# One step for each stage on each engine, and all steps placed anew, in a fused attention and expert kernel

## The reference: what is computed

```python
x = x + xattn(layernorm(x), ctx)   # 16 heads of 32; the context is key and value, then one 512 x 512 projection
x = x + attn(layernorm(x), ...)    # low-rank q, k, v with a rotation, 16 heads, 32 x 32 scores, projection
x = x + ffn(layernorm(x), ...)     # 8 experts: argmax of a gate picks one expert per row; GELU between two 512 x 512 layers
```

## Time and profile before

| what | value |
|---|---|
| median of three runs | 898.3 us |
| profiled execution: own time, span | 901.93 us, 900.0 us |
| TensorE busy, mean granted clock | 773.6 us (86% of the span), 0.926 |
| VectorE, ScalarE, GpSimd busy | 604.1, 422.1, 319.6 us |
| first scores to last scores of the 64 batches | 10.0 to 647.8 us |
| last tile's stages, then the routing | to about 714 us |
| experts | to the end, 900 us |

### The profile page before, as it was taken

The page is one execution under the profiler, slowest core; times in us unless marked ns, Lnnn a source line. Parts: engine busy times, 40 slices in busy tenths (PEclk is TensorE's granted clock), DMA queues, the critical chain, the costliest instruction groups (busy, mean ns, idle before and its releaser), DMA issues.

```text
span 900.0 us, 26139 instructions
## 1 busy us (share of the span) xinstructions
PE 773.6 (86%) x10442; PEld 573.5 (64%) x10442; DVE 604.1 (67%) x1195; ACT 422.1 (47%) x1063; POOL 319.6 (36%) x638
## 2 busy tenths in 40 slices
PE   4896988979788897978889797888979888999998
PEld 3543756758566675757667585766767665566664
DVE  3476766767776676677676677767654645678883
ACT  2353454544644455454645455454541344555552
POOL 2013333223333323233332223333230234776652
PEclk9998898989898898989889898988989889999999
DMA  9955455546646463554645465374250199654430
GB/s 265 314 133 101 135 120 119 146 98 135 151 107 145 118 154 105 121 130 96 173 114 136 98 154 130 97 176 110 35 193 32 52 355 393 210 170 141 149 120 4
DMA packets 113848, 129.05 MB, mean 143 GB/s; under 512 B 13950, under 2 KB 80766, under 8 KB 113728
## 3 DMA queue, kind: packets, MB, share of 16 engines
q1 hardware_dynamic: 105984, 109.26, 46.6%
q0 software_dynamic: 5520, 16.26, 5.3%
q10 hardware_dynamic: 2224, 1.86, 0.8%
HBM read 114.76 MB, written 14.42 MB: 144 GB/s over the span
## 4 chain that ended last, share of the span: by engine, by line
PE 55%; DVE 14%; issue 10%; POOL 8%; ACT 7%; SPq 3%; DMA 2%; ACTq 0%; POOLq 0%; DVEq 0%
PE bank L497 11%; PE bank L498 8%; PE bank L499 8%; PE bank L1551 7%; PE scores L548 3%; PE scores L538 3%; PE bank L562 3%; PE bank L491 3%; ACT prob L813 2%; POOL operand_lo L1283 2%; DVE k_block L1114 2%; PE scores L1529 2%; PE scores L1531 2%; PE scores L1530 2%; PE bank L602 2%
## 5 line engine op out<-in xcount | busy, mean ns | idle before, releaser
L813 ACT ACTIVATE prob<-scores,negmax 128x257 f32<-128x257 f32 x256 | 118.0, 476 | 85.0 <-DVE negmax L1021 84.7
L548 PE MATMUL scores<-consts,prob 128*128 128x128 f32 x512 | 89.5, 303 | 60.7 <-ACT prob L813 60.7
L1021 DVE TENSOR_REDUCE negmax<-scores 128x2 f32<-128x514 f32 x128 | 82.0, 682 | 67.4 <-PE scores L538 67.4
L548 PEld LDWEIGHTS scores<-consts,prob 128*128 128x128 f32 x512 | 67.5, 156 | 73.4 <-ACT prob L813 68.1
L497 PE MATMUL bank<-qkv_hi,operand_hi 128*128 128x396 f32 x256 | 100.1, 391 | 3.9 <-DVE operand_lo L1025 3.8
L1011 DVE STREAM_TRANSPOSE k_t<-keys 128x512 f32<-128x512 f32 x128 | 88.1, 690 | 3.1 <-DMA keys<-in_ctx 3.0
L498 PE MATMUL bank<-qkv_lo,operand_hi 128*128 128x396 f32 x256 | 89.0, 348 | 0.1
L499 PE MATMUL bank<-qkv_hi,operand_lo 128*128 128x396 f32 x256 | 88.7, 347 | 0.0
L1551 PE MATMUL bank<-w_all,hidden 128*128 x184 | 82.8, 592 | 0.6 <-ACT hidden L1604 0.6
L562 PEld LDWEIGHTS bank<-prob_t,context 128*32 128x32 f32 x4096 | 48.7, 115 | 45.5 <-issue 45.2
L1647 DVE TENSOR_TENSOR w_lo<-w_all,w_hi 128x512 fp32r<-128x512 f32 x89 | 69.5, 839 | 0.1
(11 more groups left out here) (245 smaller groups left out, 1743.2 us busy)
## 6 DMA issues: line engine op xcount, KB each, us to landing
keys<-in_ctx SPq DMA_DIRECT2D x256, 128.0 KB, 4.6
context<-in_ctx SPq DMA_DIRECT2D x64, 512.0 KB, 4.7
w_all<-in_L_ffn_W SPq DMA_DIRECT2D x16, 1024.0 KB, 10.2
b<-in_L_ffn_b SPq DMA_DIRECT2D x23, 256.0 KB
norm_scratch<-norm SPq DMA_DIRECT2D x16, 256.0 KB, 2.0
x_tile<-in_x SPq DMA_DIRECT2D x8, 256.0 KB, 4.8
x_pair<-in_x SPq DMA_DIRECT2D x8, 256.0 KB, 4.8
x_scratch<-x_tile SPq DMA_DIRECT2D x8, 256.0 KB, 2.6
```

Of the source, the lines that this page charges most:

```text
L548: done = pe.transpose(scores[:, 2 * pair, at:at + P], prob[pair][:, gg, c * P:(c + 1) * P], ident)
L813: act.activation(prob[pair][:, gg, :], scores[:, g, 0:J], ACT.Exp, bias=negmax[b % 2][:, g:g + 1], accum_out=sums[t % 2][:, g, bl:bl + 1]) ...
L1021: dve.tensor_reduce(negmax[b % 2][:, 2 * pair:2 * pair + 2], scores[:, 2 * pair:2 * pair + 2, 0:J], AX.X, ALU.max, negate=True).then_inc(m ...
```

## The change

The table of constants gets a step of its own for each stage on each engine, and parts that were spread over steps in a row (`XOUT`, `OUT`, `SOFT_PLACE`) get a tuple of steps. The fixed distances (`QKV + 4`, `TURN_Q + 1`, `AV + 2`, `RANK + 1`) are gone. All numbers are new, those inside a batch too. Which heads of k ScalarE and VectorE place is now in two names, with the values as before. No instruction is added or removed in the 16 tiles, and the code of each stage is the same.

```diff
-(INVERT, SPREAD_INV, SPREAD_LAST, WEIGH_LAST, X_BIAS, ATT, ATT_INV, ATT_HI, ATT_LO, XOUT, X1, SCALE1, TURN1, QKV, OUT_BIAS, TURN_Q, TURN_K,
- SELF, SOFT, SOFT_EXP, SOFT_SUM, SOFT_SCALE, SOFT_TURN, SOFT_PLACE, AV, OUT, X2, SCALE3, TURN3, GATE, CHOOSE, RANK,
- QUERIES) = (
-    -5, -3, 0, 1, -6, 2, 3, 4, 4, 8, 17, 19, 21, 24, 26, 41, 41, 45, 46, 46, 50, 48, 56, 55, 63, 83, 89, 86, 95, 105, 105, 118, -54)
-MEASURE_X, SCALE_X = 2 * STEPS + 4, 2 * STEPS + 5
-LATER = {"OUT": (6, 0), "X2": (12, 0), "SCALE3": (25, 8), "TURN3": (36, 0), "GATE": (28, 0), "CHOOSE": (29, 0), "RANK": (17, 0)}
+INVERT, SPREAD_INV, SPREAD_LAST, WEIGH_LAST = -5, -4, 1, -3
+ATT, ATT_INV, ATT_HI, ATT_LO = 5, 6, 4, 12
+X_BIAS, XOUT, X1, ROOT1, SCALE1 = -28, (8, 9, 11, 13), 16, 20, 18
+TURN1, NORM_HI, NORM_LO = 21, 19, 19
+QKV = tuple(range(24, 40))
+QKV_MOVE, ROTATE, OUT_BIAS = (28, 31, 36, 40), 30, 21
+TURN_Q, Q_MOVE, TURN_K, K_PLACE, K_PLACE_DVE = 44, 44, 41, 41, 45
+SELF, SOFT, SOFT_EXP, SOFT_SUM, SOFT_SCALE, SOFT_TURN, SOFT_PLACE = 46, 49, 49, 50, 56, 56, (53, 55, 60, 62)
+AV, SELF_HI, SELF_LO, OUT, X2, ROOT3 = 66, 66, 70, (81, 85, 86, 87), 89, 85
+SCALE3, TURN3, X3_MOVE, GATE, CHOOSE, RANK, RANKED = 90, 95, 96, 105, 105, 120, 120
+QUERIES, QUERIES_MOVE = -55, -54
+MEASURE_X, ROOT_X, SCALE_X = 25, 26, 30
+LATER = {'OUT': (16, -4), 'X2': (19, 0), 'SCALE3': (26, 12), 'TURN3': (29, 7), 'GATE': (38, 14), 'CHOOSE': (31, 4), 'RANK': (25, 1)}
...
-KEYS_AT = (5, 7)
-KEYS_LOAD_AT = 6
-TURN_P_AT = (6, 8)
-ATTEND_AT = (10, 12)
-KEEP_AT = (7, 9)
+KEYS_AT = (6, 7)
+KEYS_LOAD_AT = 8
+TURN_P_AT = (7, 8)
+ATTEND_AT = (10, 11)
+KEEP_AT = (7, 8)
...
-def part_at(step, offset, parts, later=(0, 0)):
-
-    for part in range(parts):
-        t = tile_at(step, offset + part, later)
+def part_at(step, offsets, later=(0, 0)):
+
+    for part, offset in enumerate(offsets):
+        t = tile_at(step, offset, later)
         if t >= 0:
             return t, part
     return -1, 0
...
-            t = tile_at(step, TURN_Q + 1)
+            t = tile_at(step, Q_MOVE)
             if t >= 0:
                 until.wait_ge(q_turned, t + 1)
...
-            t = tile_at(step, TURN_K + 1)
-            if t >= 0:
+            t = tile_at(step, K_PLACE_DVE)
+            if t >= 0 and DVE_K:
...
-            t = tile_at(step, X2, LATER["X2"])
+            t = tile_at(step, ROOT3, LATER["X2"])
             if t >= 0:
                 root("r", measured_r, t + 1, normed_r, rstd_r)
```

More of the change, by code:

```diff
@@ L367, in program @@
     bank_of = {"queries": 0, "xout": 0, "norm": 1, "qkv0": 1, "qkv2": 1, "out": 2, "gate": 0, "av": 0, "qkv1": 2, "q": 1, "k": 0, "norm3": 1, "rank": 0, "qkv3": 0, "self": 1}
-    step_of = {"queries": QUERIES, "xout": XOUT, "norm": TURN1, "qkv0": QKV, "qkv1": QKV + 4, "qkv2": QKV + 8, "qkv3": QKV + 12,
-               "q": TURN_Q, "k": TURN_K, "self": SELF, "av": AV, "out": OUT, "norm3": TURN3, "gate": GATE, "rank": RANK}
+    step_of = {"queries": QUERIES, "xout": XOUT[0], "norm": TURN1, "qkv0": QKV[0], "qkv1": QKV[4], "qkv2": QKV[8], "qkv3": QKV[12],
+               "q": TURN_Q, "k": TURN_K, "self": SELF, "av": AV, "out": OUT[0], "norm3": TURN3, "gate": GATE, "rank": RANK}
     later_of = {"out": LATER["OUT"], "norm3": LATER["TURN3"], "gate": LATER["GATE"], "rank": LATER["RANK"]}
@@ L633, in stages @@
                 turn(norm_w, bank, norm_turned)
-            t, part = part_at(step, QKV, 4 * G)
+            t, part = part_at(step, QKV)
             if t >= 0:
@@ L662, in stages @@
                 until.wait_ge(q2_moved, t + 1)
-                until.wait_ge(k_placed, 2 * t + 2)
+                until.wait_ge(k_placed, K_PARTS * (t + 1))
                 for g in range(G):
@@ L816, in stages @@
         def stages(step):
-            t = tile_at(step, QUERIES)
+            t = tile_at(step, QUERIES_MOVE)
             if t >= 1:
@@ L841, in stages @@
                 act.activation(q2_t[:, :], banks[bank_of["q"]][:, :], ACT.Copy, scale=SSCALE).then_inc(q2_moved, 1)
-            t = tile_at(step, TURN_K + 1)
-            if t >= 0:
+            t = tile_at(step, K_PLACE)
+            if t >= 0 and ACT_K:
                 until.wait_ge(k_turned, t + 1)
@@ L846, in stages @@
                 until.wait_ge(zeroed, 2)
-                for hl in (1, 3):
+                for hl in ACT_K:
                     rows = slice(hl * HD, (hl + 1) * HD)
@@ L1110, in stages @@
                 until.wait_ge(zeroed, 2)
-                for hl in (0, 2):
+                for hl in DVE_K:
                     rows = slice(hl * HD, (hl + 1) * HD)
@@ L1325, in pool_program @@
                     move_last(b + 1, 1)
-            if step % TILE == MEASURE_X and t + 1 < T:
+            if step % TILE == ROOT_X and t + 1 < T:
                 root("x", measured_x, t + 2, normed_x, rstd_x)
```

39 lines of the change are left out of this document (20 added, 19 removed).

## The result

The changed kernel takes 853.1 us (median of 4 runs, 849.76 to 856.24), beside 896.3 us for the kernel before on the same chip: a ratio of 0.953 [0.947, 0.958], 4.7% faster. The forecast was 870. The profiled execution took 849.76 us, 52.2 less than that of before; it was the fastest of its kernel's runs, and that of before was slower than all four beside it, so profiles side by side show more than the 43.2 us between the medians.

What follows compares the result with a forecast made beforehand. TensorE's work plus its waits and low-clock stretches bound the kernel. 13 turns by 2.0 us give 26, the ends 1 and 1, together 28: 874 from the profiled 901.9, 870 for the median; range 847 to 893.

Steps and rivals of the forecast that it cites:

- the case that it forecast: Whole kernel: 870 us, the clock falling once per turn as before; chance 0.50, own range 862 to 880.
- rival 1: The clock holds between self attention's scores and the projection; each turn gains 2.0 + 1.9 us, giving 845; chance 0.17.
- its own sign: Prediction wrong if a second low-clock stretch or none appears, or the high cut starts over 2.5 us after the attention's sum.
- A: Each turn from qkv's start to self attention's scores: 1.0 us lost, with 0.9 newly idle ahead of self attention.
- B: From self attention's scores to the projection, 6.9 us: idle time 5.1 to about 3.2, counting A's 0.9.
- VectorE: Its work ahead of the projection: with the spread moved into idle time, maxima and attention's sum come 0.9 us earlier.
- ScalarE: Exponentials ahead of the norm's scale start 0.75 after the maxima, 2.4 us earlier; the projection starts 2.1 us earlier.
- Part C: From the projection to the next qkv: still 13.3 us, gain or loss nothing within 0.5, if the clock behaves as before.
- Once, as before: TensorE's clock still falls once per turn, one low stretch of about 6.8 us, judged from a last-tile gap of 1.26 us.
- The rule that I set aside: Long idle gaps between matmul bursts lower throughput, short ones keep TensorE's clock up; by it the gain is 51, not 28.
- Rival 2: The clock falls a second time, in Part C: 914 if every turn, chance 0.08; 892 if about half, chance 0.13.
- Rival 3: The earlier exponentials win nothing, a new wait taking their place: 889 to 898, say 894; chance 0.12.

Runs made afterwards that it cites:

- b_scale3: Kernel before, with only the third norm's scale moved behind the four exponentials on ScalarE: 896.4 us, ratio 0.998.
- b_scale3_hi: Kernel before, with the third norm's scale behind the exponentials and the high cut ahead of self attention's exponential on ScalarE: 878.6 us, ratio 0.982.
- a_soft_exp: Changed kernel, with self attention's exponential put back ahead of the attention's high cut on ScalarE: 863.5 us, ratio 0.966.
- b_fill: Kernel before, with six unused products on TensorE filling its 3.61 us wait behind self attention's scores: 880.7 us, ratio 0.980.
- a_turn_q: Changed kernel, with the queries' turn put back beside that of the keys: 859.0 us, ratio 0.954.
- a_av: Changed kernel, with the product with the values moved ahead of the norm's turn, no longer between it and qkv: 836.6 us, ratio 0.930.
- b_part_b: Kernel before, with scale behind exponentials, high cut ahead of self attention's exponential, and VectorE's spread ahead of the move of the values: 878.1 us, ratio 0.981.

## Why the prediction was right, and where it was off

The number is right by its range, not by its case. 853.1 lies in the 847 to 893 that the prediction states, but outside the 862 to 880 of the case that it forecast; the range reached so low for the sake of rival 1. And by its own sign (wrong if "a second low stretch or none is there") the step on the clock failed, while what it said of A and B held.

*Part A.* Forecast +1.0 for a wait of 0.9 ahead of self attention. Measured +0.8 and 0.69.

*VectorE.* Forecast 0.9 from the spread. Measured 1.2 for the maxima, but from TensorE's order more than from the spread, which is worth 0.3 in the order of before and 0.1 in that of after.

*ScalarE.* The exponentials start 0.69 after the maxima (forecast 0.75) and ahead of the scale; the high cut starts 2.1 after the attention's sum (under 2.5 was asked); the first transpose follows without a wait. Projection 2.5 earlier for 2.1, 23.8 after qkv for 24.2. The new waits are where they were put, ahead of the norm's turn (1.00 for 1.3) and of the projection (0.80 for 1.0). The exponentials, though, are only the visible part: b_scale3 shows that alone they give 0.2, b_scale3_hi that the high cut adds 1.1, and a_soft_exp that in the changed kernel it gives 0.6.

*Part C.* Here the step failed. "Once, as before" was taken for the clock, with a chance of 0.50; it didn't fall in B at all, and C took the 11.4 us of rival 1 in 8 turns of 13, and 11.8 to 12.7 in the others, where 13.3 was forecast. The sum, by 13: 26 forecast, 7 more since the projection starts 2.6 and not 2.1 us earlier after qkv, 1 for small waits that weren't there, 16 from C: 50.7. So the clock's part is a third in these 13 turns, and 18 of 43 us by b_fill, not quite the half of the theory above. The place of the fall was taken from the earlier trace rows, a gap of 1.26 us in the last tile, where little other work stands around it. That row doesn't carry over to a tile in mid-stream: a_soft_exp has gaps of 1.01 and 1.41 us in B and no fall there in 13 turns. The rule that I set aside, that of the Trainium skill, page "TensorE: Matmul & The Clock Gate", section "Why this matters for your kernels", that long idle gaps between bursts of matmuls make the throughput drop, came nearer. b_fill bears it out: with the gap of 3.61 us filled, the falls in B go from 13 to none. But the shorter gaps are not safe here: b_scale3 has none over 2.3 us in B and falls in all 13 turns, and a_turn_q falls in 9 with none over 1.33. The rule gives the direction, and no run here shows a length of gap below which the clock holds.

*The rivals.* What happened is rival 1, which had 0.17: the clock holds in B. Its 53 us are the 52.2 between the profiled executions; by the medians it is 43, and 853.1 for its 845, with falls at the end of C in 4 turns, about 1.1 us each, as the part of the difference that the trace shows. Rival 2's mechanism (falls in C) is real in those 4 turns, where it needed all 13 or about half, and without a fall in B beside it. Rival 3 is what b_scale3 shows when the scale is moved alone: 896.4.

*Small slips.* The rule's 51 leaves out the 2 us of the ends that rival 1's 53 has, and so isn't set against 28 on the same footing. The chances as given add up to 0.75 for faster and 0.08 for slower, for 0.76 and 0.09.

*Open.* What decides whether the clock falls in a turn. B's waits sort the kernels only roughly: 1.70, 1.05 and 0.80 us give 10 falls, 1.33, 1.05 and 0.80 give 9, 1.34 and 1.21 give 4, 1.01 and 1.41 none. Turns of one kernel with the same waits differ. Nor is it shown why a_av has fewer falls at the end of C; its idle time in C is 1.07 us in this turn, for 1.46. And the changes of `OUT`, `TURN_P_AT` and `XOUT` on TensorE were not run one by one; what a_turn_q leaves of the 0.9 us is their sum with all else that b_part_b lacks.
